# Down product of the two shared units in three fp32r terms, in a Macaron layer

## The reference

```
x = x + 0.5 * ffn(layernorm(x))
x = x + attention(layernorm(x))
x = x + 0.5 * ffn(layernorm(x))      # the same weights as the first

# ffn: 8 experts of 128, top 2 with a capacity, and two shared units of 128
comb = top-2 weights of softmax(x @ gate_w.T), zero past the capacity
y    = sum over e of comb[:, e] * ((silu(x @ we_gate[e].T) * (x @ we_up[e].T)) @ we_down[e].T)
sh   = (silu(x @ ws_gate.T) * (x @ ws_up.T)) @ ws_down.T
ffn  = y + sh
```

## Time and profile before

| | us |
|---|---|
| median of 3 runs | 1348.82 |
| lowest and highest | 1347.32, 1349.87 |
| the profiled execution | 1350.99 |
| its span | 1349.2 |
| TensorE busy | 1273.4 |
| VectorE busy | 823.9 |
| ScalarE busy | 614.0 |
| GpSimd busy | 883.1 |

### The profile page before, as it was taken

One profiled execution on the slowest core, in us unless ns is written; L12 is line 12 of the kernel. 1 busy time (PEld: TensorE's weight loads), 2 busy tenths in 40 slices (PEclk: granted clock), 3 DMA queues, 4 the chain that ended last, 5 costly groups with the idle time before them and its releaser, 6 DMA issues.

```text
span 1349.2 us, 21617 instructions
## 1 busy us (share of the span) xinstructions
PE 1273.4 (94%) x7858; PEld 796.0 (59%) x7858; DVE 823.9 (61%) x1352; ACT 614.0 (46%) x917; POOL 883.1 (65%) x652
## 2 busy tenths in 40 slices
PE   5999997699999999999999999999999983999998
PEld 3666664456666565656565656566666542666665
DVE  6656646776666666666666766666666522665632
ACT  3443432345455545455545455554545431433422
POOL 0533445578888887888788887888788830343343
PEclk9999999799999999999999999999999995999999
DMA  5343031123232332232332323232323210332140
GB/s 159 126 173 127 15 112 31 32 44 70 52 70 55 66 60 61 64 57 59 62 72 50 72 49 72 49 72 49 72 53 68 57 19 14 126 134 73 69 149 16
DMA packets 118680, 95.39 MB, mean 71 GB/s; under 512 B 75760, under 2 KB 85008, under 8 KB 118320
## 3 DMA queue, kind: packets, MB, share of 16 engines
q1 hardware_dynamic: 118576, 94.01, 28.0%
HBM read 57.53 MB, written 2.88 MB: 45 GB/s over the span
## 4 chain that ended last, share of the span: by engine, by line
PE 86%; DVE 6%; issue 3%; ACT 2%; DMA 2%; POOL 1%; SPq 0%; DVEq 0%; ACTq 0%; POOLq 0%
PE banks L965 17%; PE banks L431 13%; PE banks L948 13%; PE banks L442 9%; PE banks L980 7%; PE banks L924 6%; PE banks L889 6%; PE banks L953 4%; PE banks L989 4%; PE banks L908 3%; PE banks L931 1%; DVE neg_max L1110 1%; PE banks L393 1%; PE banks L386 1%; DMA rec_d<-rec_c 1%
## 5 line engine op out<-in xcount | busy, mean ns | idle before, releaser
L1110 DVE TENSOR_REDUCE neg_max<-banks 128x2 f32<-128x1024 f32 x256 | 313.3, 1224 | 105.6 <-PE banks L924 99.7
L1046 ACT ACTIVATE work<-banks 128x1024 f32<-128x1024 f32 x256 | 250.4, 1025 | 171.2 <-PE banks L953 171.2
L1194 POOL TENSOR_TENSOR turn<-turn,side_turned 128x512 f32<-128x512 f32 x128 | 160.7, 1277 | 131.8 <-DMA side_turned<-side 131.8
L965 PE MATMUL banks<-work 128*64 128x512 f32 x1024 | 234.6, 600 | 0.0
L544 ACT ACTIVATE o_t<-banks 128x512 f32<-128x512 f32 x160 | 95.4, 596 | 196.0 <-PE banks L431 193.2
L1188 POOL TENSOR_TENSOR turn<-turn,fenc 128x512 f32<-128x512 f32 x128 | 161.8, 1287 | 16.0 <-DVE side L1103 12.3
L1199 POOL TENSOR_TENSOR qk_l<-turn,qk_h 128x512 fp32r<-128x512 f32 x128 | 162.0, 1288 | 2.3 <-ACT qk_h L1051 2.3
L1204 POOL TENSOR_TENSOR work<-work 128x1024 f32<-128x1024 f32 x64 | 152.8, 2388 | 6.7 <-PE banks L965 6.7
L965 PEld LDWEIGHTS banks<-work 128*64 128x64 f32 x1024 | 68.0, 137 | 133.7 <-issue 111.3
L734 POOL TENSOR_TENSOR turn<-turn,work 128x512 f32<-128x512 f32 x56 | 72.3, 1293 | 99.4 <-DVE turn L670 99.4
L924 PE MATMUL banks<-qk_h 64*128 64x512 f32 x512 | 117.7, 454 | 11.3 <-DVE neg_max L1110 8.3
(11 more groups left out here) (162 smaller groups left out, 2301.2 us busy)
## 6 DMA issues: line engine op xcount, KB each, us to landing
work<-share SPq DMA_DIRECT2D x32, 1024.0 KB, 9.2
side_turned<-side SPq DMA_DIRECT2D x256, 128.0 KB, 3.1
rec_all<-rec_d SPq DMA_DIRECT2D x128, 128.0 KB, 3.1
x_tok<-in_x SPq DMA_DIRECT2D x8, 256.0 KB, 6.3
out<-x_tok SPq DMA_DIRECT2D x8, 256.0 KB, 9.2
work<-in_w_gate_up SPq DMA_DIRECT2D x1, 1280.0 KB, 7.3
work<-in_w_qk SPq DMA_DIRECT2D x1, 1024.0 KB, 7.8
den_d<-den_rows SPq DMA_DIRECT2D x64, 4.0 KB
```

The costliest lines, as they stand in the source:

```text
L965: ins = nc.tensor.matmul(O[OWN[h], :], v_all[:, kt, n * DH:(n + 1) * DH], pt[:, g % 2, kt, h * T:(h + 1) * T], start=(kt == 0), stop=(kt = ...
L1046: nc.scalar.activation(pt[:, g % 2, kt, :], S[kt].rearrange("p h q -> p (h q)"), ACT.Exp, scale=QSCALE).then_inc(s["probs"], 1)
L1110: nc.vector.tensor_reduce(neg_max[:, g % 2, qt::DH], M2, AX.X, ALU.max, negate=True).then_inc(s["maxes"], 1)
L1194: nc.gpsimd.tensor_tensor(turn[:, g % 2, part], turn[:, g % 2, part], side_turned[:, part], ALU.add).then_inc(done, 1)
```

## The change

High and low parts are made of the down weights and of the gated rows of the two shared units, and used in the down product:

- `down_hi` and `down_lo`: the down weights of the two shared units, split by ScalarE (`down_high`) and VectorE (`down_low`) in period 0 of the first stage. All later numbers of `w_hi_ready` and `w_lo_ready` go up by one.
- `hid_hi` and `hid_lo`: the gated row of a shared unit, split by ScalarE (`hidden_high`, an activation of 128x512, in the period after the unit's own, behind the next silu) and by GpSimd (`hidden_low`, a subtraction of 128x512, in the unit's place in its queue, where it had nothing to do for shared units).
- `down(i)` makes three fp32r products in place of one fp32 product when g is 0 or 1, and waits for `hid_lo_ready` in place of `gated`. Experts are left as they were.
- `hidden_high` also waits until the down product of the last unit with the same g has read the tile: there is one pair of tiles for each g.

The hunks that only raise a semaphore's number for the attention weights, and the two new semaphore names, are left out here:

```diff
--- before.py
+++ after.py
@@ -99,6 +99,8 @@
         gu_hi = sb("gu_hi", [P, 2 * GROUPS, P], F32R)
         gu_lo = sb("gu_lo", [P, 2 * GROUPS, P], F32R)
         down_w = sb("down_w", [P, GROUPS, D])
+        down_hi = sb("down_hi", [P, NSH, D], F32R)
+        down_lo = sb("down_lo", [P, NSH, D], F32R)
         gate_w = sb("gate_w", [P, E])
         gate_hl = sb("gate_hl", [P, 2 * CB, GATE_ROWS], F32R)
         qk_hi = sb("qk_hi", [P, PAIRS, QK, P], F32R)
@@ -166,6 +168,7 @@
         den_d = nc.dram_tensor("den_d", (B * PAIRS, 4, T // 2), F32).ap()
         rec_d = nc.dram_tensor("rec_d", (B * PAIRS, 2, T), F32).ap()
         fourier_s, fproj_s = turn[0:NF, 0, 0, :], turn[0:NF, 0, 1, 0:P]
+        hid_hi, hid_lo = qk_h[:, 1], qk_l[:, 1]
         hid_later = [turn[:, 1, 0], turn[:, 1, 1], o_raw[:, 0], o_raw[:, 1]]
         hid_first = [work[:, n * T:(n + 1) * T] for n in range(6)] + hid_later
         xn2 = [xn, sb("xn_odd", [P, TT, D])]
@@ -232,6 +235,14 @@
             nc.scalar.activation(gate_up_part(gu_hi[:].rearrange("p g n -> p (g n)"), n), gate_up_part(st_gu, n),
                                  ACT.Copy).then_inc(w_hi_ready, 1)
 
+        def down_high(act):
+            act.wait_ge(in_down, 16)
+            nc.scalar.activation(down_hi[:], down_w[:, 0:NSH], ACT.Copy).then_inc(w_hi_ready, 1)
+
+        def down_low(dve):
+            dve.wait_ge(w_hi_ready, 3)
+            nc.vector.tensor_tensor(down_lo[:], down_w[:, 0:NSH], down_hi[:], ALU.subtract).then_inc(w_lo_ready, 1)
+
         def setup_dve(dve):
             nc.vector.memset(ones_b[:], 1.0).then_inc(consts_ready, 1)
             nc.vector.memset(gate_hl[:].bitcast(F32), 0.0).then_inc(consts_ready, 1)
@@ -248,7 +259,7 @@
             ins.then_inc(w_lo_ready, 1)
 
         def gate_up_low(dve, n):
-            dve.wait_ge(w_hi_ready, 2 + n)
+            dve.wait_ge(w_hi_ready, 2 + 2 * n)
             hi, lo = (gate_up_part(w[:].rearrange("p g n -> p (g n)"), n) for w in (gu_hi, gu_lo))
             nc.vector.tensor_tensor(lo, gate_up_part(st_gu, n), hi, ALU.subtract).then_inc(w_lo_ready, 1)
 
...
@@ -336,6 +347,9 @@
 
             def experts(i):
                 return sum(1 for b, g in UNITS[0:i] if g >= NSH)
+
+            def shared(i):
+                return sum(1 for b, g in UNITS[0:i] if g < NSH)
 
             def last_of(b):
                 return max(i for i in range(N) if UNITS[i][0] == b)
@@ -424,7 +438,7 @@
                     b, g = UNITS[i]
                     pe.wait_ge(s["x_lo_ready"], b + 1)
                     if not last and g == PART and b == 0:
-                        pe.wait_ge(w_lo_ready, 3)
+                        pe.wait_ge(w_lo_ready, 4)
                     for dst, j, read, done in ((G[i % 2], g, "silu", "gate_ps"), (U[i % 2], GROUPS + g, "gated", "up_ps")):
                         at_least(pe, s[read], i - 1)
                         for m, (w, a) in enumerate(((gu_hi, xh), (gu_lo, xh), (gu_hi, xl))):
@@ -433,14 +447,19 @@
 
                 def down(i):
                     b, g = UNITS[i]
+                    if i == first_of(b):
+                        at_least(pe, s["y_copied"], b - 1)
                     if g < NSH:
-                        pe.wait_ge(s["gated"], i + 1)
+                        pe.wait_ge(s["hid_lo_ready"], shared(i + 1))
+                        if not last and i == 0:
+                            pe.wait_ge(w_lo_ready, 3)
+                        for n, (w, a) in enumerate(((down_hi, hid_hi), (down_lo, hid_hi), (down_hi, hid_lo))):
+                            ins = nc.tensor.matmul(Y[b % 2], w[:, g, :], a[:, g, :], start=(i == first_of(b) and n == 0),
+                                                   stop=False)
                     else:
                         pe.wait_ge(s["weighted"], experts(i + 1))
-                    if i == first_of(b):
-                        at_least(pe, s["y_copied"], b - 1)
-                    nc.tensor.matmul(Y[b % 2], down_w[:, g, :], hid(i), start=(i == first_of(b)),
-                                     stop=(i == last_of(b))).then_inc(s["down"], 1)
+                        ins = nc.tensor.matmul(Y[b % 2], down_w[:, g, :], hid(i), start=False, stop=(i == last_of(b)))
+                    ins.then_inc(s["down"], 1)
 
                 def transpose_y(b):
                     pe.wait_ge(s["y_copied"], b + 1)
@@ -543,6 +562,12 @@
                     at_least(act, s["gated"], i - 1)
                     nc.scalar.activation(act_g[:, i % 2, :], G[i % 2][:], ACT.Silu).then_inc(s["silu"], 1)
 
+                def hidden_high(i):
+                    b, g = UNITS[i]
+                    act.wait_ge(s["gated"], i + 1)
+                    at_least(act, s["down"], max((n for n in range(i) if UNITS[n][1] == g), default=-1) + 1)
+                    nc.scalar.activation(hid_hi[:, g, :], hid(i), ACT.Copy).then_inc(s["hid_hi_ready"], 1)
+
                 def copy_y(b):
                     act.wait_ge(s["down"], last_of(b) + 1)
                     at_least(act, s["yt_ps"], b)
@@ -552,6 +577,10 @@
                     if i < N:
                         silu(i)
                     c, q = chunk(i)
+                    if 0 <= i - 1 < N and UNITS[i - 1][1] < NSH:
+                        hidden_high(i - 1)
+                    if not last and i == 0:
+                        down_high(act)
                     if not last and i == REST_AT:
                         gate_up_high(act, 1)
                     if batch_at(i, FRONT_AT) is not None:
@@ -685,6 +714,8 @@
                     if i < N:
                         gated(i)
                     c, q = chunk(i)
+                    if not last and i == 0:
+                        down_low(dve)
                     if not last and i == REST_AT:
                         gate_up_low(dve, 1)
                     if turned_at(i) is not None:
@@ -725,6 +756,12 @@
 
             def pool(pool):
 
+                def hidden_low(i):
+                    b, g = UNITS[i]
+                    pool.wait_ge(s["hid_hi_ready"], shared(i + 1))
+                    nc.gpsimd.tensor_tensor(hid_lo[:, g, :], hid(i), hid_hi[:, g, :], ALU.subtract)\
+                        .then_inc(s["hid_lo_ready"], 1)
+
                 def weighted(i):
                     b, g = UNITS[i]
                     if (g - NSH) % HALF_E == 0:
@@ -738,6 +775,8 @@
                 for i in range(N):
                     if UNITS[i][1] >= NSH:
                         weighted(i)
+                    else:
+                        hidden_low(i)
 
             def sync(sp):
 
@@ -751,7 +790,7 @@
                     if b >= 2:
                         sp.wait_ge(s["weighted"], experts(last_of(b - 2) + 1))
                     elif not last and b == 1:
-                        sp.wait_ge(w_lo_ready, 3)
+                        sp.wait_ge(w_lo_ready, 4)
                     for h in range(2):
                         of = share_d[c, b % CB, :, HALF_E * h:HALF_E * (h + 1), :].unsqueeze(0)
                         sp.dma_start(share[b % 2][:, h], of.broadcast_to([P, TT, HALF_E, P]))\
...
```

More of the change, by code:

```diff
@@ L316, in ffn @@
                 "normed", "xn_ready", "xn_first", "xt_ps", "x_hi_ready", "x_lo_ready", "logits_t", "logits_copied", "logits", "shifted", "exps", "masks", "pos",
-                "routed", "turned", "rows_ready", "gate_ps", "up_ps", "silu", "weighted", "gated", "down", "y_copied", "yt_ps", "x_done")}
+                "routed", "turned", "rows_ready", "gate_ps", "up_ps", "silu", "weighted", "gated", "hid_hi_ready", "hid_lo_ready", "down", "y_copied", "yt_ps", "x_done")}
             listed = tuple(sem(f"{tag}_listed{c}") for c in range(CHUNKS))
@@ L797, in attention @@
             HALF = T // 2
-            W_ALL = 3 + PAIRS + 2
+            W_ALL = 4 + PAIRS + 2
             FILL_FROM = -2 * PAIRS
@@ L824, in qk_low @@
             def qk_low(dve, b):
-                dve.wait_ge(w_hi_ready, b + 4)
+                dve.wait_ge(w_hi_ready, b + 5)
                 pair = bass.ds(b, 1)
@@ L834, in early_pe @@
                 if k == EARLY_K:
-                    pe.wait_ge(w_lo_ready, 4)
+                    pe.wait_ge(w_lo_ready, 5)
                     pe.wait_ge(s["x_lo_ready"], 1)
@@ L865, in early_dve @@
                     cols = slice((k - 1) * T, k * T)
-                    dve.wait_ge(w_hi_ready, 3 + PAIRS + k)
+                    dve.wait_ge(w_hi_ready, 4 + PAIRS + k)
                     nc.vector.tensor_tensor(v_lo[:, cols], st_v[:, cols], v_hi[:, cols],
```

## The result

The changed kernel takes 1374.45 us (median of 4 runs) against 1348.07 us for the kernel before on the same chip: a ratio of 1.0198, 95% interval 1.0181 to 1.0216, slower by some 26 us. Forecast were 1366.8 us and at most 1374.0. The direction and the holds of VectorE came out as argued; the size did not.

What follows compares the result with a forecast made beforehand. TensorE's queue order was taken as the bound, except where VectorE's norm and routing bind. Terms 7.4 + 4.4 + 2.2 + 1.9 + 1.6 + 3.0 - 2.5 = 18.0 us gave 1366.8 us, range 1351 to 1374 us.

Steps and rivals of the forecast that it cites:

- the new wait of the down product: TensorE's shared down products: result wanted 6.8 us after gate and up, needing some 4.4 us, so no delay.
- the holds at the steps named: VectorE's L634 and L638 in routing, L273 or L275 in the norm, stretched by GpSimd's subtractions to about 1.3 us.
- the prediction's premise: VectorE instructions with both inputs in SBUF don't finish while GpSimd reads SBUF: 1.34 us against 0.22.
- Routing: Four windows of chunks 2 and 3: TensorE starts 1.85 us later in each, 7.4 us (4.4 to 10.4).
- norm of chunks 2 and 3: Layer norm in four windows: the shift arrives 1.1 us later in each, 4.4 us.
- the first masks: First mask of each feed-forward stage later: +2.2 us (0.5 to 3.0) in stage one, +1.9 us (0 to 2.6) in two.
- the clock: Half speed behind longer stops in chunks 2 and 3 and stage two: 3.0 us, between 0 and 6.0.
- Rival C: In all stops the clock falls, and VectorE's holds are full: 24 us, 1372.8 us; 12%.
- Rival B: Only the mask waits grow, the norm term absorbed by ScalarE's and TensorE's slack: 7.7 us, 1356.5 us; 22%.
- D: Whole kernel: losses and gain cancel; 4% as a rival, 5% for same in the range.
- The norm of chunk 1: Both stages: unit 3's subtraction meets a small norm step, 0.8 us each, 1.6 us (0 to 2.4).
- The kept gain: TensorE's shorter shared down products: 16 of 32 keep 0.1575 us each, 2.5 us (0 to 5.0).

Runs made afterwards that it cites:

- e1: Changed kernel without GpSimd's 32 subtractions, the third product reading the high row again: 1344.41 us, ratio 0.9988 to the kernel before.
- e2: Changed kernel with copies, subtractions and weights' split kept, but the one fp32 down product of before: 1375.34 us, ratio 1.0208 to the kernel before.
- e3: Changed kernel with the subtraction over only 256 of 512 columns, the third product reading the high row: 1355.44 us, ratio 1.0057.
- e4: Changed kernel with GpSimd setting the low row to zero once in place of the subtraction: 1346.22 us, ratio 0.9991.
- e10: Changed kernel with GpSimd setting the low row to zero three times in a row in place of the subtraction: 1346.50 us, ratio 0.9999.
- e5: Changed kernel with 20 small fp32r products ahead of each mask wait of chunks 2 and 3, 12 ahead of the first mask: 1364.75 us, ratio 1.0124.
- e9: Kernel before, with 12 small fp32r products ahead of the first mask wait of stage one: 1347.21 us, ratio 1.0003.
- e11: Changed kernel with copies, subtractions and three products only in batches 3 and 5: 1359.91 us, ratio 1.0103.
- e12: As e8, no moved units, three products only in batch 6; stage one's first stop filled with 12 products, stage two's start with 28: 1345.22 us, 0.9990.
- e7: Changed kernel with shared units moved behind the sixth expert in batches 3, 4, 5, 7, and one fp32 product in batches 0 to 2: 1351.52 us, 1.0027.
- e8: As e7, with the split of the down weights moved from period 0 to period 19 of stage one: 1352.06 us, ratio 1.0033.
- e6: Changed kernel with copies, subtractions and three products only in batches 2 to 7: 1366.75 us, ratio 1.0142.

## Why the prediction was wrong in its size

**Right.** The bound (TensorE, except where VectorE's norm and routing end last), the gain that is mostly lost, the new wait of the down product that doesn't bind (TensorE has no wait for GpSimd's subtraction in either stage), and the holds at the steps named. The instructions held were the neighbours of those named: L632 and L634 in the routing, not L634 and L638; in the norm L268 once and L272 three times, not L273. L272 has one input tile, and by the prediction's premise, two inputs in SBUF, it would not have been held. Routing, norm of chunks 2 and 3 and the first masks were forecast at 15.9 us and measured 17.4. e1 and e2 show that the subtractions carry the loss, e3, e4 and e10 that it is by their reads and for as long as they last.

**The step that failed** is the clock: "With one row on each side I take the middle, 3.0 us", with 6.0 as the upper end. All four stops of 3.4 us in the changed kernel were followed by the half clock, and against e5 the stretches behind them are 1.56, 1.48, 2.61 and 1.56 us longer, 7.2 us together; the first mask of stage two adds 1.1. That is over 8 us. Two things were off. I took the mean of falling and not falling, where the nearest row for a stop of over 3 us was the one of 2.11 us, behind which the clock had fallen. And I priced a slow stretch at 2.4 us, 1.2 us for each. The kernel before has half speed from 27.9 to 31.3 us, some 3.4 us, all behind the end of its stop, and filling that stop gave back 1.55 us there (e9). Its windows:

```profile
30.00:31.00 1.00, 1.00 (x4) 0.79 (x3) 1.00 (x8) 0.00 (x0) 0.00 (x0) 0.50 0.00 0
...
31.40:32.00 0.60, 0.60 (x5) 0.40 (x4) 0.56 (x5) 0.50 (x1) 0.00 (x0) 1.00 0.00 0
```

Behind the first of the four stops it is again 3.4 us, all of it while TensorE has work. Rival C, with a fall behind every stop and 1372.8 us, was within 2 us of the time, in part by luck: its 6.0 us for the clock were 2 us short, and its 3 us for full holds 1.5 too many. Rival B left the clock out although its stops are as long as the forecast's. And D has 4% among the rivals and 5% in the range.

**Left out.** The hand-over to attention: its first layer norm is made in VectorE's queue at units 70 to 74, beside the subtractions of 70 and 71, and TensorE's wait for it grew from 0.9 to 2.1 us. It is 0.9 again in e11 and e12, which have no subtraction at units 70 and 71; which hold makes the difference stays open. Net of the kept gain, the way from the last shares to attention is 0.5 us longer, nowhere in the sum.

**Too high.** The norm of chunk 1, 1.6 us forecast, 0.3 measured; TensorE was late itself there by the first mask. The kept gain of 2.5 us is in the right place (0.3 and 0.7 us behind the last shares of the stages, 0.3 behind each mask), but e1, at 1.6 us in all, holds 0.5 us of the weights' split against it, and half a microsecond more stays unexplained, which e1's interval (0.4 to 3.0 us) allows.

What stays open is what decides whether the clock falls, and for how long. In chunks 2 and 3 it fell behind 0 of 4 stops of 1.3 us in the kernel before, 6 of 12 of 2.1 to 2.5 us (e3, e7, e8), and 14 of 16 of 3.3 to 3.4 (changed kernel, e2, e6, e11). At the first mask of stage one it fell behind all five stops of 2.1 us (the kernel before, e4, e6, e10, e11). So the length of the stop alone doesn't decide. At the first mask of stage two it was down behind a stop of 1.40 us in the changed kernel, where TensorE had stood 1.33 us shortly before, and not behind the 1.41 us of e2, where it had not. Half speed began between 0.9 us before and 1.4 us after the end of a stop. It lasted some 3.4 us in most cases, and about twice that behind two stops of the changed kernel (the first of stage one and that of chunk 2 in stage two), one in e2 and two in e6.

## What to carry to other kernels

Work put on an idle GpSimd is not free for VectorE: look for VectorE instructions that read SBUF, two tiles above all, and sit on a bound chain, and keep GpSimd's reading instructions away from them, also those that a reordering pulls in. An idle slot on one engine may be what lets another run. Price a stop of TensorE with the slow stretch behind it, in full, as soon as a shorter stop in the same trace shows one; here 14 of 16 had it. And look at how much the part that the change doesn't touch varies between executions before a difference is read there.

## What was not expected of the hardware

VectorE's conversion (L660 of the kernel before, 1.26 us beside a product of GpSimd) and its tensor_scalar steps, which have one SBUF tile as input, are held by GpSimd's reading instructions as well: 1.29 us for L283 in the norm above and 1.09 us for L678 in the rows of e10, where 0.16 to 0.17 is usual. The Trainium skill (SBUF — State Buffer, "Who interferes with whom") has this too: copies, casts and tensor_scalar can contend when they use the second pair of ports. And more work made TensorE's part shorter: 104 added products of 256 columns in e5 took 7.2 us off the stretches behind four stops.
